# Cross-attention on one core: the keys of a batch projected in three works of up to 482 columns, where four of 361 stood

## What is computed

```python
Q = relu(x @ Wq + bq)          # (16, 100, 128)
K = relu(ctx @ Wk + bk)        # (16, 1444, 128)
V = relu(ctx @ Wv + bv)
scores = einsum('hbqd,hbkd->hbqk', Qh, Kh) / sqrt(8)
scores = where(key_mask == 0, NEG, scores)   # key_mask: rows of ctx whose sum is not 0
attn = softmax(scores) * q_mask
out = einsum('hbqk,hbkd->hbqd', attn, Vh) + x
```

## Time and profile before

| | us |
|---|---|
| median of 3 runs | 361.71 |
| lowest and highest of them | 358.92, 361.80 |
| the profiled execution, its own time | 359.1 |
| span of the profiled execution, first to last instruction | 357.2 |

### The profile page before, as it was taken

The page is one execution under the profiler, slowest core; times in us unless marked ns, Lnnn a source line. Parts: engine busy times, 40 slices in busy tenths (PEclk is TensorE's granted clock), DMA queues, the critical chain, the costliest instruction groups (busy, mean ns, idle before and its releaser), DMA issues.

```text
span 357.2 us, 16853 instructions
## 1 busy us (share of the span) xinstructions
PE 348.3 (98%) x6706; PEld 243.5 (68%) x6706; DVE 236.8 (66%) x777; ACT 300.5 (84%) x397; POOL 7.3 (2%) x30
## 2 busy tenths in 40 slices
PE   8799999999999999999999999999999999999994
PEld 5557676776767677676767767676776767677662
DVE  7768786684939568493956849395774939579321
ACT  1578698988889898888989888888988888898993
POOL 6010000000000000000000000000000000000000
PEclk9999999999999999999999999999999999999999
DMA  5947749685754737375473737547373844537000
GB/s 161 340 107 261 249 166 354 187 291 141 276 148 167 216 127 252 91 276 148 167 216 127 253 90 279 145 167 225 131 239 90 289 136 172 174 115 232 10 9 7
DMA packets 40398, 64.55 MB, mean 181 GB/s; under 512 B 28084, under 2 KB 29364, under 8 KB 40372
## 3 DMA queue, kind: packets, MB, share of 16 engines
q1 hardware_dynamic: 39442, 63.26, 55.0%
q10 hardware_dynamic: 930, 0.90, 0.7%
HBM read 13.73 MB, written 0.82 MB: 41 GB/s over the span
## 4 chain that ended last, share of the span: by engine, by line
PE 95%; DVE 2%; ACT 1%; issue 1%; ACTq 0%; DVEq 0%
PE psum L634 36%; PE psum L610 29%; PE psum L556 14%; PE psum L547 13%; PE psum L725 1%; DVE k_raw L836 1%; PE psum L708 1%; PE psum L719 1%; PE psum L720 0%; DVE late_low L1083 0%; ACT probs L515 0%; ACT query_bd L500 0%; DVE k_high L855 0%; PE psum L577 0%; DVE v_biased L879 0%
## 5 line engine op out<-in xcount | busy, mean ns | idle before, releaser
L515 ACT ACTIVATE probs<-psum 121x800 f32<-121x800 f32 x384 | 293.3, 841 | 40.9 <-PE psum L610 40.9
L634 PE MATMUL psum<-probs,values 121*32 121x200 f32 x3072 | 153.6, 333 | 0.0
L634 PEld LDWEIGHTS psum<-probs,values 121*32 121x32 f32 x3072 | 96.0, 110 | 42.1 <-issue 18.7
L610 PEld LDWEIGHTS psum<-query_bd,k_parts 64*121 64x121 f32 x1536 | 91.8, 181 | 45.2 <-issue 37.8
L610 PE MATMUL psum<-query_bd,k_parts 64*121 64x200 f32 x1536 | 115.8, 281 | 1.0 <-DVE v_biased L879 0.8
L836 DVE TENSOR_SCALAR_CACHE_REDUCE k_raw<-psum,bk_sb 128x361 f32<-128x361 f32 (+2 forms) x63 | 37.6, 599 | 79.2 <-PE psum L547 79.2
L556 PE MATMUL psum<-wv_sb,keyT 128*32 128x129 f32 (+1 forms) x1536 | 54.9, 277 | 0.0
L547 PE MATMUL psum<-keyT,wk_mixed 128*32 128x361 f32 (+2 forms) x504 | 51.6, 484 | 0.0
L889 DVE TENSOR_SCALAR values<-v_biased,keep 121x128 f32<-121x128 f32 x192 | 43.2, 283 | 6.3
L556 PEld LDWEIGHTS psum<-wv_sb,keyT 128*32 128x32 f32 (+1 forms) x1536 | 38.0, 108 | 7.2 <-issue 0.9
L879 DVE TENSOR_TENSOR v_biased<-psum,bv_sb 121x384 f32<-121x384 f32 x64 | 35.1, 548 | 0.0
(11 more groups left out here) (81 smaller groups left out, 78.6 us busy)
## 6 DMA issues: line engine op xcount, KB each, us to landing
k_parts<-k_high SPq DMA_DIRECT2D x30, 722.0 KB, 4.5
k_parts<-k_low SPq DMA_DIRECT2D x30, 722.0 KB, 5.5
keyT<-in_ctxT SPq DMA_DIRECT2D x15, 722.0 KB, 4.2
query_rep<-late_high SPq DMA_DIRECT2D x2, 600.0 KB, 7.7
query_rep<-late_low SPq DMA_DIRECT2D x2, 600.0 KB, 7.8
residual<-in_x SPq DMA_DIRECT2D x64, 12.5 KB
k_parts<-k_high SPq DMA_DIRECT2D x2, 480.0 KB, 5.0
k_parts<-k_low SPq DMA_DIRECT2D x2, 480.0 KB, 3.9
```

Source lines behind the costliest of these rows:

```text
L515: nc.scalar.activation(probs[0:KTILE, u % PROB_SLOTS], scores_ps[0:KTILE, u % SCORE_SLOTS, :, 0:QCOLS], ACT.Exp, scale=SCALE).then_inc(pro ...
L610: mm = nc.tensor.matmul(scores_ps[0:KTILE, u % SCORE_SLOTS, j, n * TCOLS:(n + 1) * TCOLS], k_parts[rows, parity, t, kt * KTILE:(kt + 1) * ...
L634: mm = nc.tensor.matmul(spans[c * VCOLS:(c + 1) * VCOLS, half, :, :, 0:SPAN], values[0:KTILE, parity, kt, half * HALF_PAIRS + c, :], probs ...
```

## The change

Three key works stand where four stood (`KPARTS`), two of 482 columns and one of 480. The last cycle of batches 1 to 13 has no side work. In batch 0 the fourth key work of batch 1 leaves cycle 2, that of batch 2 leaves cycles 6 and 7, and `low_late_queries` stands ahead of the last key read of batch 2.

```diff
-    KPARTS = 4
-    KCOLS = SK // KPARTS
-    assert KPARTS * KCOLS == SK and KCHUNKS <= KPARTS
+    KPARTS = 3
+    KCOLS = -(-SK // KPARTS)
+    assert KCOLS <= BANK and KCHUNKS <= KPARTS and VGROUPS + KPARTS <= KT * 2 // SCORE_SLOTS
...
-                    mm = project_keys(work_ps, parity, k * KCOLS, (k + 1) * KCOLS)
+                    mm = project_keys(work_ps, parity, k * KCOLS, min((k + 1) * KCOLS, SK))
...
-            SIDE_WORK = tuple((step,) for step in VALUES + KEYS)
-            FIRST_SIDE_WORK = (((0, NEXT),), ((1, NEXT), (2, NEXT)), ((3, NEXT), VALUES[0]), VALUES[1:2],
-                               VALUES[2:3], (VALUES[3], KEYS[0]), KEYS[1:3], (KEYS[3], (ROWS, NEXT)))
+            SIDE_WORK = tuple((step,) for step in VALUES + KEYS) + ((),)
+            FIRST_SIDE_WORK = (((0, NEXT),), ((1, NEXT), (2, NEXT)), VALUES[0:1], VALUES[1:2],
+                               VALUES[2:3], (VALUES[3], KEYS[0]), KEYS[1:2], (KEYS[2], (ROWS, NEXT)))
...
-                read_keys(2, 2, used + 2)
                 low_late_queries()
-                read_keys(2, 3, used + 3)
+                read_keys(2, 2, used + 2)
```

More of the change, by code:

```diff
@@ L1011, in first_batch @@
                 read_keys(2, 1, used + 1)
+                low_late_queries()
                 read_keys(2, 2, used + 2)
-                low_late_queries()
-                read_keys(2, 3, used + 3)
                 used = used + KPARTS
```

## The result

The changed kernel takes 368.98 us (median of 6 runs, 368.71 to 371.01), the kernel before 360.45 (median of 6, 358.92 to 362.92). The ratio is 1.0247, with a 95% interval from 1.0195 to 1.0298: slower, by 8.5 us on the medians and well clear of no change; whether it is slower by more than 2% the interval leaves open. The forecast was 369.0. Its own sum, though, was +7.3 us from profile to profile, 366.4, and the changed kernel's profiled execution takes 368.84, which is +9.7 over the 359.1 of before. So the first question is whether the forecast 7.3 us are there, the second where the rest comes from.

A forecast was written before the change was run, and what follows sets the result against it. Bound by TensorE's columns, ScalarE not far behind; moved columns sum to nought, the wait gives 13 x 0.55 = +7.15 us, batch 0 +0.15, together +7.3; on the median 361.7 that is 369.0, range 365.0 to 371.0.

The forecast's parts named there:

- What a column costs: TensorE's key works: 1.67 ns a column, fixed price near nothing; 361 added columns cost +0.603 us on cycles 4 to 6.
- rival B: Key works have a fixed price after all, added columns cost 0.41 us: +4.8 in all, 366.5; chance 0.09.
- rival C: The longer key works cost more, 2.3 ns a column: +10.4 in all, 372.1; chance 0.04.
- The new wait: After empty cycle 7, TensorE waits for ScalarE at the next cycle's third score unit: 0.55 us a batch.
- rival A: The third unit's slot is free in time, so no wait; only batch 0's +0.15 is left, 361.9; chance 0.10.
- The sum over the loop: Batches 1 to 13 each take 0.55 us longer: 13 x 0.55 = +7.15 us.
- VectorE: VectorE's read before the second value work isn't late: its slack of 0.11 us grows, as TensorE is held up 0.55.
- Batch 0: Longer key works and their reads: +0.13 us up to the first value work, +0.01 to the row pick, taken as +0.15.

The follow-up runs named there:

- Experiment 2: Changed kernel with a fourth key work in cycle 7 that projects columns 0 to 361 again: 368.73 us, ratio to the kernel before 1.0238.
- experiments 5 and 6: ScalarE's exponential over only 400 of a unit's 800 columns, on the changed kernel (364.39 us) and on the kernel before (356.81 us).
- Experiment 4: Changed kernel with its empty cycle moved to cycle 4 and the key works in cycles 5 to 7: 370.67 us, ratio to the kernel before 1.0292.
- experiment 1: The kernel before, run again unchanged for a second profile: 362.01 us.
- experiments 7 to 10: Changed kernel with padding instructions, first costly (medians 376.67, 374.51 us), then in TensorE's idle stretch plus VectorE's pads (367.63), and repeated without pads (369.36).
- experiment 7: Changed kernel with 17 one-column matmuls (68 rows and weight loads) added at the start of TensorE's stream: median 376.67 us.
- experiment 8: Changed kernel with 17 one-column matmuls at the start of TensorE's stream and 14 one-column memsets at the start of VectorE's: median 374.51 us.

## Why the prediction was right, and where luck helped

- *What a column costs.* Forecast 1.67 ns, the three works together +0.603 us. Experiment 2 measured +0.60. Right: rival B falls, and rival C, the works at 2.3 ns a column, with it. The 60 cycles of overhead a matmul that the Trainium skill states ("TensorEngine Tiling (Array Packing)", section Instruction Overhead) don't show in this stream of four column strips: by the prediction's estimate 8 rows fewer a batch would save 0.20 us, and experiments 5 and 6, whose batches have the same columns in rows that differ by these 8, took 20.78 and 20.79.
- *The new wait.* Forecast 0.55 us in the next batch's cycle 0, at the third unit, released by ScalarE; measured 0.54, at that place, in each batch of the loop. Experiments 5 and 6 show its cause by taking it away, and rival A, a slot that is free in time, falls with it. The forecast rested on one place of the profile of before, batch 14's cycle 4, which had the very pattern that the change makes, and on the 0.08 by which ScalarE starts later in cycle 7. Experiment 4 confirms both: in cycle 4 the wait is 0.46, in cycle 7 0.54.
- *The sum over the loop.* Forecast 13 x 0.55 = 7.15, measured 13 x 0.53 = 6.9.
- *VectorE.* Forecast: its slack grows in the changed kernel. It does, to 283.82 - 282.97 = 0.85 us. Experiment 4 shows that the slack of 0.11 was real, and what happens without the stand.
- *Batch 0.* Forecast +0.15. From the first key work to the first value work it now takes 6.62 us for 6.38, +0.24 (forecast +0.13). The second key work starts 1.98 us after the first, 0.33 more than before, as forecast; the third starts 1.87 after the second where 1.55 stood, 0.12 more than its columns: it too waits for the read ahead of it now, which the forecast didn't count. From cycle 5's key work to the row pick it is 6.60 for 6.65 (forecast +0.01). Together +0.2.
- *What the sum lacked.* The two breaks behind the loop, 2.9 us, are in no term of it. Padded, the changed kernel's lowest time is 366.34, and the forecast on the profile's base was 366.4. That 369.0 met the median of 368.98 is luck. The sum was put on the median of the runs shown, 361.7, which lies 2.6 us above the profiled execution. Breaks like the one of experiment 1 and stretches at the lower clock make such executions; which it was in those runs is not on record. The changed kernel, whose fastest execution took 368.7, has 2.9 us of other breaks in both its profiles. A like amount was added, for a wrong reason.

## What to carry to other kernels

When two engines alternate through a few buffers, what counts is not the busy share but the shortest time between two visits to the buffers: here TensorE could come back after 2.58 us but not after 1.97, because ScalarE needs 0.73 a unit for three units and a start. Side work laid evenly between such visits fills time that the slower engine needs anyway; the same work laid in fewer, larger pieces costs its full columns where it goes and gives almost nothing back where it leaves (0.07 us of 0.60 here). Look in the profile for a stretch that already has the new pattern, and take its numbers rather than the average. And before a difference of under 1% is put down to a change, look for breaks that end with "issue", whose place can depend on the count of instructions alone, and for stretches at the lower granted clock.

## What was not expected of the hardware

- Two breaks of 1.18 and 2.32 us that stay with a certain length of the instruction streams and go when 68 TensorE and 14 VectorE instructions are put ahead (experiments 7 to 10). Like the one of 2.41 us that came by chance (experiment 1), they end 1.35 to 1.48 us after a transfer of the kind "instruction".
- The granted clock can fall to its lower level, 0.50, in one execution of a kernel and stay at 1.00 in another: 3.2 us between the two profiles of the changed kernel.
- A one-column matmul is not cheap by being one column. With a 128-column stationary operand the 34 rows took 7.25 us in experiment 7, 0.21 a row, and 4.30 in experiment 8. There the rows up to 6.05 us start 0.21 apart, and behind 6.1 us, where the clock's record at 1.00 begins, they start 0.11 apart. With a one-column stationary operand, at 1.00, 34 rows took 0.99, 0.03 a row. The streamed column is the same, only the stationary operand differs, and its loads (PEld) start as far apart as the rows:

```profile
5.13 7.25 PE L727 MATMUL psum<-ones 128*128 128x1 f32 x34
```

```profile
5.13 4.30 PE L728 MATMUL psum<-ones 128*128 128x1 f32 x34
```

```profile
11.39 0.99 PE L748 MATMUL psum<-ones 128*1 128x1 f32 x34
```
